# Four-layer adaLN network on one core: exponentials of two recurrences moved ahead of an expert loop, and their reciprocals split between ScalarE and VectorE

## The reference, cut to what matters

```python
ek  = exp(min(k, 30));  ekv = ek * v
a = a * decay + ekv                                # scanned forwards and backwards over time
b = b * decay + ek
euk = exp(min(u + k, 30))
num = nf + nb - ekv + euk * v
den = df + db - ek + euk
cond = sigmoid(x) * (num / max(den, 1e-8)) * (0.8 + 0.2 * tf)
x = x + ffn(cond)
```

## Time and profile before

| | |
|---|---|
| median of 3 runs | 438.07 us |
| profiled execution: its time | 438.29 us |
| profiled execution: span from first to last instruction | 436.6 us |
| busy share of the span | PE 89%, DVE 75%, POOL 57%, ACT 53% |
| mean granted TensorE clock | 0.975 of full speed |
| share of the chain that ended last | PE 52%, DVE 29%, issue 8%, DMA 4%, ACT 4%, POOL 1% |

### The profile page before, as it was taken

One profiled execution on the slowest core, in us unless ns is written; L12 is line 12 of the kernel. 1 busy time (PEld: TensorE's weight loads), 2 busy tenths in 40 slices (PEclk: granted clock), 3 DMA queues, 4 the chain that ended last, 5 costly groups with the idle time before them and its releaser, 6 DMA issues.

```text
span 436.6 us, 6831 instructions
## 1 busy us (share of the span) xinstructions
PE 389.6 (89%) x2025; PEld 244.8 (56%) x2025; DVE 327.8 (75%) x620; ACT 232.9 (53%) x462; POOL 248.0 (57%) x347
## 2 busy tenths in 40 slices
PE   7898999999899999975895899999999999886895
PEld 7676788655455555643685445455445545563463
DVE  5998798999999999979887456654855452068993
ACT  5724594466676766757785423232322323259792
POOL 5475008489678998424840655785687366124641
PEclk9999999999999999999995699999999999999998
DMA  6910003455465644329311277926975710330011
GB/s 205 411 64 0 2 1 148 179 189 171 170 222 198 210 166 162 127 81 368 132 50 48 79 261 244 389 92 233 328 233 192 279 39 14 96 128 0 24 38 36
DMA packets 27347, 65.57 MB, mean 150 GB/s; under 512 B 3360, under 2 KB 7840, under 8 KB 26672
## 3 DMA queue, kind: packets, MB, share of 16 engines
q1 hardware_dynamic: 24320, 58.93, 38.9%
q0 software_dynamic: 1904, 5.18, 3.8%
q10 hardware_dynamic: 1088, 1.05, 0.7%
HBM read 102.83 MB, written 4.78 MB: 247 GB/s over the span
## 4 chain that ended last, share of the span: by engine, by line
PE 52%; DVE 29%; issue 8%; DMA 4%; ACT 4%; POOL 1%; SPq 1%; DVEq 0%; POOLq 0%; ACTq 0%
PE bank L2055 14%; PE bank L2089 8%; PE bank L1822 7%; DVE hx L1341 4%; DVE fw L1130 4%; DVE bw L1133 3%; PE bank L1667 3%; PE bank L1668 3%; PE bank L1669 3%; DVE fw L1138 2%; DMA dn<-in_dn 2%; PE bank L2066 2%; PE bank L1919 2%; DVE xp L1399 2%; PE bank L1744 2%
## 5 line engine op out<-in xcount | busy, mean ns | idle before, releaser
L2055 PE MATMUL bank<-gu,xbT 128*64 128x512 f32 (+1 forms) x320 | 71.3, 583 | 1.2 <-ACT xbT L964 0.9
L1822 PE MATMUL bank<-hx,w2raw 128*128 128x512 f32 x128 | 67.3, 607 | 4.6 <-DVE hx L1341 3.8
L852 ACT ACTIVATE rl<-bank 128x512 f32<-128x512 f32 x64 | 38.1, 595 | 38.3 <-PE bank L1669 37.5
L1562 DVE TENSOR_TENSOR hm<-bank,sl 128x512 f32<-128x512 f32 (+1 forms) x20 | 13.5, 675 | 48.8 <-issue 31.8
L1667 PE MATMUL bank<-xlhi,w1hi 128*128 128x512 f32 x64 | 49.3, 771 | 0.0
L2055 PEld LDWEIGHTS bank<-gu,xbT 128*64 128x64 f32 x320 | 25.9, 137 | 33.8 <-issue 28.8
L1341 DVE TENSOR_TENSOR hx<-bank,cwb 128x512 f32<-128x512 f32 x64 | 42.0, 659 | 3.1 <-ACT bank L856 3.0
L1138 DVE RECIPROCAL fw<-fw 128x256 f32<-128x256 f32 x23 | 39.8, 1730 | 0.0
L2089 PE MATMUL bank<-dn,hT 128*64 128x256 f32 x304 | 37.0, 384 | 2.7 <-ACT hT L976 0.3
L856 ACT ACTIVATE bank<-rl 128x512 f32<-128x512 f32 x64 | 38.1, 597 | 0.0
L634 POOL DMA_INDIRECT y_rows<-yb,dest_i x19 | 21.4, 1126 | 22.8 <-ACT yb L983 21.6
(11 more groups left out here) (312 smaller groups left out, 913.5 us busy)
## 6 DMA issues: line engine op xcount, KB each, us to landing
gu<-in_gu SPq DMA_DIRECT2D x86, 512.0 KB
dn<-in_dn SPq DMA_DIRECT2D x43, 512.0 KB
cwb<-cw_rows SPq DMA_DIRECT2D x32, 512.0 KB, 4.1
traw<-in_t SPq DMA_DIRECT2D x3, 1024.0 KB, 7.4
w1raw<-in_w SPq DMA_DIRECT2D x8, 256.0 KB, 4.7
w2raw<-in_w SPq DMA_DIRECT2D x8, 256.0 KB, 4.3
kT<-in_kt SPq DMA_DIRECT2D x4, 256.0 KB, 5.5
x<-in_x SPq DMA_DIRECT2D x2, 512.0 KB, 7.2
```

The costliest lines, as they stand in the source:

```text
L852: act.activation(rl[:, u % 3, :], bank[u % 4][:], ACT.Relu).then_inc(sem("r_ready"), 1)
L1822: pe.matmul(bank[4 + s][:], w2raw[:, e // 4 % 2, e % 4, :], hx[:, 0, u % 4, :], start=(e == 0), stop=(e == E0 - 1), skip_group_check=True) ...
L2055: ins = pe.matmul(bank[2 * (b % 2) + up][part(g), inner(b)], xbT[:, b % 2, k, part(g)], rhs, start=(k == 0), stop=(k == KC - 1))
```

## The change

The exponentials: POOL adds and clips for all 16 recurrences of layers two and three in one run of 16 instructions (`wkv_kup(l, blk)`), which waits until layer one's last gain has been transposed (`G_turned` 4), because it writes into the buffer `GT` that layer one used. ACT then takes the exponential of a whole layer in one instruction of 128x2048 (`wkv_exp(l)`, two of them). The single steps in the expert loop go.

The reciprocals: for n from 8 to 23 ACT takes inverse root and square (`loop_inverse`), and DVE does `loop_product`, `loop_step` and `loop_gain`, with the intermediate value in half of a PSUM bank (`newton_bank`). The sign that the Newton step leaves is taken out by a column of `tfb`. ACT loads one more table before the loop.

```diff
+EXTRA = (5, 8, 11, 14)
+FIRST_OF = [4 * (q - 2) + sum(e < q for e in EXTRA) for q in range(2, 2 * EG + 1)]
...
+        def unit_eu(n):
+
+            q = n - NBLK
+            return GT[:, (1 + q % 2) % 2, q // 2, :]
+
+        def newton_bank():
+
+            return bank[7][:, S:2 * S]
...
-            def wkv_kup(n, l, blk):
-
-                if n >= NBLK + 2:
-                    pool.wait_ge(sem("sum_num"), n - 1)
-                pool.tensor_scalar(eu[:, n % 2, 1, :], kT[:, blk, :], ubk[:, l, blk // KC, blk % KC:blk % KC + 1], 30.0, ALU.add, ALU.min
+            def wkv_kup(l, blk):
+
+                pool.tensor_scalar(GT[:, l % 2, blk, :], kT[:, blk, :], ubk[:, l, blk // KC, blk % KC:blk % KC + 1], 30.0, ALU.add, ALU.min
                                    ).then_inc(sem("kup_ready"), 1)
...
             split_w1(0)
+            pool.wait_ge(sem("te_sum"), 2)
+            pool.wait_ge(sem("G_turned"), 4)
+            for l in (1, 2):
+                for blk in range(NBLK):
+                    wkv_kup(l, blk)
             split_w1(1)
             for q in range(2 * EG):
                 wkv_sums(NBLK + q, q // 2, q % 2)
-                if q + 2 < 2 * EG:
-                    wkv_kup(NBLK + q + 2, 1 + q % 2, q // 2 + 1)
...
-            def wkv_exp(n, p):
-
-                act.wait_ge(sem("kup_ready"), n - NBLK + 1)
-                act.activation(eu[:, p, 1, :], eu[:, p, 1, :], ACT.Exp).then_inc(sem("eu_ready"), 1)
+            def wkv_exp(l):
+
+                act.wait_ge(sem("kup_ready"), NBLK * l)
+                act.activation(GT[:, l % 2, :, :], GT[:, l % 2, :, :], ACT.Exp).then_inc(sem("eu_ready"), 1)
...
+            def loop_inverse(n):
+
+                p, done = n % 2, 2 * (n - DIVIDED)
+                act.wait_ge(sem("sum_den"), n + 1)
+                act.activation(eu[:, p, 1, :], fw[:, p, 1, :], ACT.Abs_reciprocal_sqrt, bias=tiny[:],
+                               scale=2.0 ** -14).then_inc(sem("r0_ready"), 1)
+                act.wait_ge(sem("r0_ready"), done + 1)
+                act.activation(eu[:, p, 1, :], eu[:, p, 1, :], ACT.Square, scale=2.0 ** -7).then_inc(sem("r0_ready"), 1)
...
             load_table(4, ACT.Exp)
-            wkv_exp(NBLK, 0)
-            wkv_exp(NBLK + 1, 1)
+            wkv_exp(1)
             expert_relu(0)
             expert_square(0)
-            expert_relu(1)
             for s in range(2):
...
-            wkv_exp(NBLK + 2, 0)
+            wkv_exp(2)
+            expert_relu(1)
+            act.activation(table[:, 3:4], tiny[:], ACT.Abs_reciprocal_sqrt)
+            loop_inverse(NBLK)
             for u in range(1, UNITS):
                 if u + 1 < UNITS:
                     expert_relu(u + 1)
                 expert_square(u)
-                if u % 4 == 0 and u // 4 + 2 < 2 * EG:
-                    wkv_exp(NBLK + u // 4 + 2, u // 4 % 2)
+                if u - 1 in FIRST_OF:
+                    loop_inverse(NBLK + 1 + FIRST_OF.index(u - 1))
                 if u == UNITS - 3:
                     latent_copy(0)
...
+            def loop_product(n):
+
+                dve.wait_ge(sem("r0_ready"), 2 * (n - DIVIDED) + 2)
+                dve.wait_ge(sem("G_ready"), n)
+                dve.scalar_tensor_tensor(out=newton_bank(), in0=eu[:, n % 2, 1, :], scalar=1e8, in1=fw[:, n % 2, 1, :],
+                                         op0=ALU.min, op1=ALU.mult).then_inc(sem("newton"), 1)
...
+            def loop_step(n):
+
+                dve.wait_ge(sem("newton"), 2 * (n - DIVIDED) + 1)
+                dve.scalar_tensor_tensor(out=loop_quotient(n), in0=newton_bank(), scalar=2.0, in1=eu[:, n % 2, 1, :],
+                                         op0=ALU.subtract, op1=ALU.mult).then_inc(sem("newton"), 1)
+
+            def loop_gain(n):
+
+                dve.wait_ge(sem("sum_num"), n + 1)
+                dve.wait_ge(sem("newton"), 2 * (n - DIVIDED) + 2)
+                dve.scalar_tensor_tensor(out=unit_eu(n), in0=loop_quotient(n), scalar=-1e8, in1=fw[:, n % 2, 0, :],
+                                         op0=ALU.max, op1=ALU.mult).then_inc(sem("G_ready"), 1)
...
                     wkv_scan(n, l, blk, p, j)
-                    if j == 1:
-                        gain_reciprocal(n - 1, 1 - p)
+                    if q > 1 and j == 2:
+                        loop_product(n - 1)
+                    if q > 1 and j == 3:
+                        loop_step(n - 1)
                     if q > 1:
                         expert_h(u)
                         u += 1
-                    if j == 2:
-                        gain_out(n - 1, 1 + (q - 1) % 2, (q - 1) // 2, 1 - p)
+                    if q > 1 and j == 3:
+                        loop_gain(n - 1)
...
             for u in range(UNITS - 4, UNITS):
                 expert_h(u)
-                if UNITS - 4 <= u < UNITS - 2:
-                    last_reciprocal(u - UNITS + 4)
+                if u == UNITS - 3:
+                    loop_product(3 * NBLK - 1)
+                if u == UNITS - 2:
+                    loop_step(3 * NBLK - 1)
             add_routed(0)
             add_routed(1)
-            gain_out(3 * NBLK - 1, 2, NBLK - 1, 1)
+            loop_gain(3 * NBLK - 1)
```

More of the change, by code:

```diff
@@ L517, in wkv_sums @@
             def wkv_sums(n, blk, p):
[L519 to L522, removed]
+                wait_alone("eu_ready", 1 + (n - NBLK) % 2)
+                pool.tensor_tensor(eu[:, p, 0, :], unit_eu(n), kT[:, blk, :], ALU.mult).then_inc(sem("euv_ready"), 1)
                 for d, part in ((1, "den"), (0, "num")):
@@ L528, in wkv_sums @@
                     wait_alone("both_" + part, n + 1 - NBLK)
-                    pool.tensor_tensor(fw[:, p, d, :], fw[:, p, d, :], eu[:, p, d, :], ALU.add).then_inc(sem("sum_" + part), 1)
+                    pool.tensor_tensor(fw[:, p, d, :], fw[:, p, d, :], unit_eu(n) if d else eu[:, p, 0, :], ALU.add
+                                       ).then_inc(sem("sum_" + part), 1)
             def split_side(k):
@@ L548, in _ @@
             first_value(6)
-            pool.wait_ge(sem("te_sum"), 2)
-            wkv_kup(NBLK, 1, 0)
             first_value(7)
-            wkv_kup(NBLK + 1, 2, 0)
             def split_w1(eg):
@@ L666, in _ @@
                 gather_block(b)
-            pool.wait_ge(sem("eu_ready"), 2 * NBLK + 1)
+            pool.wait_ge(sem("eu_ready"), 3)
             late_value(0)
@@ L1134, in wkv_scan, with loop_quotient @@
                                            0.0, ALU.add, ALU.mult).then_inc(sem("scan_num" if part == 3 else "scan_den"), 1)
+            def loop_product(n):
[3 more added lines that the diff above has]
+                                         op0=ALU.min, op1=ALU.mult).then_inc(sem("newton"), 1)
+            def loop_quotient(n):
+                return eu[:, n % 2, 1, :] if n == 3 * NBLK - 1 else newton_bank()
+            def loop_step(n):
[7 more added lines that the diff above has]
+                                         op0=ALU.max, op1=ALU.mult).then_inc(sem("G_ready"), 1)
             def gain_reciprocal(n, p):
@@ L1142, in gain_out @@
                 dve.wait_ge(sem("sum_num"), n + 1)
-                dve.wait_ge(sem("rden_ready"), n + 1 - NBLK + DIVIDED)
+                dve.wait_ge(sem("rden_ready"), n + 1 - 3 * NBLK + DIVIDED)
                 dve.scalar_tensor_tensor(out=GT[:, l % 2, blk, :], in0=fw[:, p, 1, :], scalar=1e8,
@@ L1154, in make_cond @@
                 dve.scalar_tensor_tensor(out=cond[:, 2 * b:2 * b + 2, :], in0=gain_bank(l, b)[:].rearrange("p (t c) -> p t c", t=2),
-                                         scalar=tfb[:, 1 if l == 0 and KC * b >= DIVIDED else 3, b:b + 1],
+                                         scalar=tfb[:, 1 if l in (1, 2) or l == 0 and KC * b >= DIVIDED else 3, b:b + 1],
                                          in1=cond[:, 2 * b:2 * b + 2, :],
@@ L1342, in expert_h @@
                                   ).then_inc(sem("h0_ready"), 1)
-            def last_reciprocal(half):
-                cols = slice(half * P, half * P + P)
-                dve.wait_ge(sem("sum_den"), 3 * NBLK)
-                ins = dve.reciprocal(fw[:, 1, 1, cols], fw[:, 1, 1, cols])
-                if half:
-                    ins.then_inc(sem("rden_ready"), 1)
             chain(dve.tensor_copy(bank[7][:, 0:2 * NBLK], dec[:, 1:3, :, :].rearrange("p l b k -> p (l b k)")))
@@ L1358, in _ @@
                 n, l, blk, p = NBLK + q, 1 + q % 2, q // 2, q % 2
+                if q > 1:
+                    assert u == FIRST_OF[q - 2]
                 for j in range(4):
                     wkv_scan(n, l, blk, p, j)
-                    if j == 1:
-                        gain_reciprocal(n - 1, 1 - p)
+                    if q > 1 and j == 2:
+                        loop_product(n - 1)
+                    if q > 1 and j == 3:
+                        loop_step(n - 1)
                     if q > 1:
@@ L1365, in _ @@
                         u += 1
-                    if j == 2:
```

(5 more changed lines are left out.)

## The result

The changed kernel takes **432.12 us** (median of 6 runs, 429.79 to 432.6) against 436.71 for the kernel before (6 runs, 436.08 to 438.12): a ratio of 0.988, 95% interval 0.9858 to 0.9902. It is 1.2% faster. I had forecast 438.4 and no change, counted from the 438.07 of three runs. What happened is rival 1, which had 431.3. In the profiled execution the time is 432.6 and the span 430.9 us, 5.7 less than in the profile before.

The account below looks back on a forecast made before the run. DVE was taken to bound the expert loop, PE after the change; 438.29 - 7.8 (loop) + 1.0 (its end) + 6.3 (clips) + 0.8 (clock) = 438.6 profiled, hence 438.4; own range 435.5 to 441, whole range 430.8 to 443.0.

Parts of the forecast that it names:

- rival 1: Routing beside the clips: clips do not hold DVE up, or two links pass per stop; 431.3 us, chance 0.28.
- The loop, 7.8 us less: Expert loop: with reciprocals and gains off DVE, PE becomes the bound at 94.2 us instead of 102.0.
- The product's stretch: New DVE product in the loop, two SBUF inputs: may stretch from 0.41 to 0.60 us, 14 times.
- The end of the loop, +1.0: Last inverse and square on ACT delay the last squares and layer two's sigmoid: +1.0 us (0.5 to 1.2).
- The run of clips, +6.3: Routing ahead of the loop: POOL's clips hold up DVE's chain, making PE 6.3 us late (0 to 7.8).
- the slack of 4.8 us: Between the routing's end at 61.95 and PE's transposition of its result at 66.75: delay up to 4.8 us is covered.
- one link passes at each stop: Routing chain on DVE: one of 13 links passes per POOL instruction, 13 x 1.2 = 15.4 us.
- The clock, +0.8: PE idle for 6.3 us ahead of the loop may lower its clock: +0.8 us, middle of none and 1.7.
- rival 2: PE's wait lowers its clock during shared_down: above 440.3 from 5 us on, 448 for all of it; chance 0.20.
- Rival 3: Loop misses PE's pace because ACT waits for POOL's denominator sum; half the gain lost, 442.3 us, chance 0.09.

Follow-up runs that it names:

- Experiments 5 and 6: Two halves of the change: 5, exponentials ahead, reciprocals on DVE as in kernel before, 436.98 us; 6, reciprocals moved, exponentials one at a time as before, 455.66 us.
- experiment 4: Changed kernel with third shared-branch addition ahead of round 2, last inverse behind the last square, its DVE instructions behind the routed additions: 429.1 us.
- experiment 3: Changed kernel without the run of clips, ACT taking the two long exponentials straight from k: 432.22 us.
- experiment 1: Changed kernel with the 16 clips replaced by 28 sums of two tensors of the same 128x256: 438.49 us.

## Why the prediction was wrong, step by step

- **The loop, 7.8 us less: right.** 7.68 in the trace, PE-bound as worked out (94.36 us for 94.2), and no wait for ACT that PE would feel in place of the reciprocal. Experiments 5 and 6 show that the gain, but for some 1.2 us, is the reciprocals', made possible by the exponentials. The product's stretch was estimated at 0.2 us a time and was 0.27 (mean 0.675 for 0.41), at no cost with DVE off the bound.
- **The end of the loop, +1.0: right.** 1.1 at the sigmoid; experiment 4 takes 0.85 of it back by moving the inverse.
- **The run of clips, +6.3: wrong, and the step that decided.** "The bounds: nothing, if a clip leaves DVE alone, and one clip's length for each link of the routing chain. I take the upper one, because the nearest rows, a sum beside a two-input gain and beside a small tensor_scalar, both block to the end." A clip blocks, but lets DVE go after 0.33 of its 1.14 us, and only four links meet that part of one: the chain is 0.62 us longer, not 11, and the slack of 4.8 us takes it. What reaches y(0) is 0.3 us (experiment 3). That one link passes at each stop, and the slack, were sound: with sums in the run (experiment 1) the chain ends at 71.45, PE waits, and the time is 438.49.
- The rows that I took as nearest were near in operands and far in what counted. A sum's hold-up and its length lie so close (0.60 and 0.74 us) that "to the end" and "for the columns read" are easily taken for each other. I also misread: the gain ended 0.28 us after the sum, which I called its bare work, but that is 0.41, so DVE was let go 0.13 us before the sum's end. The other warning I put in rival 1 alone: a clip takes 1.23 us where a sum with results as wide takes 0.73, so a clip may well spend most of its time on something else than what holds DVE up.
- The Trainium skill, page "SBUF — State Buffer", section "Who interferes with whom", has a two-input VectorE instruction contend with any GpSimd instruction that reads SBUF. The traces agree that all five forms contend. The page's section "SBUF: two separate sides" also gives the ports that the two share, for the whole instruction, to the one that starts first; here the measurement differs, 0.33 of 1.14 us for a clip and 0.55 of 2.00 for a wide one.
- **The clock, +0.8:** did not arise, since PE did not wait for the routing; the granted clock is 1.00 from 62 to 80. Where PE did wait, in experiment 1, it fell to 0.50, as rival 2 had it, for some 6.9 us (its "two low stretches, 6.8 us") and not for all of shared_down. From the transposition to y(0) PE then took 15.34 us instead of 13.24: 2.1 us, where I had allowed 0.8.
- **Rival 1: right** in that the chain lands inside the slack, though a clip does hold DVE up, if briefly. That its 431.3 lies so near to 432.1 is partly luck: its fall of 6.8 us was counted from 438.07, the median of three runs, and six give 436.71; the sigmoid came 6.25 us earlier, and the medians fell by 4.6. Rival 3, a loop that doesn't reach PE's pace, did not happen: the loop's mean is 94.36 / 60 = 1.57 us a unit, against PE's own 1.56.
- Three of its sums are off without consequence: 13 x 1.2 is 15.6, not 15.4; 14 x 0.2 is 2.8, not 2.7; and rival 2 passes 440.3 from 5.4 us of low clock on (437.6 + 5.4 / 2), not from 5.

## What to carry to other kernels

Price contention between two engines by how long the other's instruction holds the shared resource, not by how long it lasts, and do not carry a price from one form of instruction to another without a row of that form; where a bound of the range decides the sign, put the chance between the ends. Background work beside a latency-bound chain should be of the kind that holds seldom: the same 20 us of POOL cost the routing 0.6 us as clips and 9.5 us as sums. And when an edit's halves look separate, ask what each needs from the other: here the exponentials went ahead to keep ScalarE on one table, and without that the reciprocals alone are 4.5% slower.

## What the runs showed of the hardware that I had not expected

POOL's 128x256 instruction with add and minimum takes 1.14 us and that with multiply and add 0.48, yet both hold a DVE instruction up equally long, 0.33 us from their start. With sums of two tensors the hold-up follows the columns read as well: 0.32 us for twice 128, 0.60 for twice 256.
